# Parts of projections, merged stack transfers, earlier transposes, other engines for additions and roots, in a one-core attention kernel

## The chip, the cores and the metric

One core of one Trainium2 chip runs the program. The metric is device time in microseconds (us), the median of several executions. The engines are TensorE (PE; its weight loads are PEld), VectorE (DVE), ScalarE (ACT), GpSimd (POOL) and SyncE (SP), which here issues all transfers. TensorE's clock has two levels, 1.2 and 2.4 GHz; a granted clock of 0.50 is the lower one throughout a stretch, 1.00 the upper.

## The reference

A block of two layers with a layer norm behind each, on x of 4 batches x 2048 rows x 256, in float32:

```python
# layer 1: 16 heads of 16; the weights of a row are summed over m and multiply that row's own v
x_proj = (x @ w_in.T + b_in).reshape(b, l, 16, -1)
q, k, v = jnp.split(x_proj, 3, axis=-1)
att = softmax(jnp.einsum('blhd,bmhd->blmh', q, k) * scale, axis=2)
opt = jnp.einsum('blmh,blhd->blhd', att, v).reshape(b, l, d)
x = layernorm(x + opt @ w_out.T + b_out)
# layer 2: a router picks 4 of 16 heads of 64 for each batch
dist = softmax(jnp.mean(x @ Wr + br, axis=1)); idx = sort(top_k(dist, 4))
Qs, Ks, Vs = (x @ W + bias) of the four heads
O = softmax(Qs @ Ks.T / 8) @ Vs
x = layernorm(x + O @ Wo + bo)
```

## The kernel before, in words

**Layer 1 as tiles.** The softmax weights of a row m multiply v of row l alone, so a head needs only the largest score of a row and the sum of its exponentials. A *tile* A(b, j) is 128 rows x 1024 columns of one head: two matmuls of 96 x 512 in bf16 into a pair of PSUM banks (line 796), VectorE's minimum over 1024 columns (line 1083), ScalarE's exponential with a running sum (line 920). There are 512 tiles a batch, 32 a head. q and k stand in three bf16 levels each in a scratch tensor in DRAM, `qk_levels`; a head's operand, the *stack*, is six blocks of 16 rows for q and six for k (levels 0, 0, 0, 1, 1, 2 and 0, 1, 2, 0, 1, 0), loaded by 12 transfers (the "LS" unit, lines 566 to 579) into one of two buffers.

**Projections.** x comes in chunks of 512 rows: XT transposes a chunk on TensorE (line 769; ScalarE copies it out, line 926), QP and KP project to 128 columns of q or k (one PSUM bank, float32, line 775, read at lines 1089 and 932), VP to v (a pair of banks, 16 matmul records, line 761, read at line 1099). "LV" splits q and k into levels, on POOL or, for the first half of batch 0, on VectorE (lines 630 to 636). "SV" stores them.

**Between the layers.** When a batch's tiles are done, OT transposes, OP projects (line 761), VectorE adds and takes statistics (lines 1059 to 1069), ScalarE makes 1/sqrt(var) by a logarithm and an exponential, each with a table load ("LN", lines 972 and 974), a Newton step and the scaling follow ("NM", lines 643 to 652; VectorE, or POOL for the FO norms of batches 0 to 2), X1 transposes back. RT is the router; "LW" loads the chosen heads' weights.

**Layer 2.** Eight groups of 16 steps a batch. S is a score pair of 128 x 1024 for the row maxima (PE line 858, DVE 1162), M turns maxima into rows, T is the transposed score with the maximum taken off (PE 873 and 876, ACT exponential 990), V multiplies by the values (PE 886, accumulates four steps in one bank; ScalarE copies the bank out, line 1000, POOL adds it to `oacc`, line 726). POOL sums the exponentials (`facc`, lines 717 and 720). D sums `facc` over partitions (line 894), R spreads the reciprocal (line 901), VectorE multiplies (line 1182), FO projects (line 761). FK, FQ and FV are the projections of layer 2.

**The order.** All queues have a fixed order, worked out by `plan()`, an event simulation with a cost for every unit. `work_lists()` gives TensorE five lists, `main`, `scores`, `products`, `inputs` and `tiles`, each unit with a *spot*, a number of about the batch and its fraction. Whenever TensorE is free in the simulation, it takes among the five list heads that are ready and for which banks are free the one with the lowest spot (lines 294 to 306). PSUM is a ring of eight banks: A, S, T, XT, VP, FV, OP, FO, OT, X1 take a pair, QP, KP, FK, FQ, D, R, M one, V one for four steps. The tiles of batch b + 1 run beside layer 2 of batch b; batch 0's tiles run beside all projections of all batches (spots -1 to 0 for the tiles, 84 input units over -0.97 to -0.07); the last batch's layer 2 runs alone. The other engines take their units in the order in which the simulation made them ready.

```python
                    if n in pe_ready and (not banks_of[n] or pick(banks_of[n])):
                        key = spot
                        if best is None or key < best[0]:
                            best = (key, i, n)
```

## Time and profile before

| | |
|---|---|
| median of 3 runs | 4086.33 us (4085.86 to 4088.03) |
| the profiled execution | 4086.6 us, span 4084.8 us |
| busy PE, DVE, ACT, POOL | 3616.2, 3287.2, 3098.1, 1662.8 us |
| DVE tile minimum (line 1083) | 2048 x 1216 ns |
| ACT tile exponential (line 920) | 2048 x 1094 ns |

The page has, for each engine, the busy time and, for each group of instructions, the count, the mean duration and the idle time ahead of it with what ended it. Durations of instructions that follow one another overlap a little: back to back, VectorE's minima come every 1.11 to 1.13 us. Stages, by time: 0 to 57 start; 57 to 760 batch 0's tiles with all projections; then three times a junction and a middle (about 915 us a batch); 3490 to 3640 the last junction; then the last batch's layer 2.

### The profile page before, as it was taken

The numbers are of one execution on the slowest core, as the hardware profiler recorded it, in microseconds if no ns is written. First come the engines' busy times: TensorE is split into PE (matmuls) and PEld (weight loads), VectorE is DVE, ScalarE is ACT, GpSimd is POOL, SyncE is SP. The second block draws the span as 40 slices with busy tenths as digits, with TensorE's granted clock in tenths as the row PEclk, the third lists the DMA queues.
The fourth block names the chain that finished last, engine by engine and source line by source line (L and its number), as shares of the span: only waits on it lengthen the run. The fifth ranks groups of instructions, "written<-read, shape, count | busy, mean of one in ns | idle before, by whom it ended". The sixth has DMA issues, their size and how long they took to land.

```text
span 4084.8 us, 41654 instructions
## 1 busy us (share of the span) xinstructions
PE 3616.2 (89%) x13992; PEld 1329.7 (33%) x13992; DVE 3287.2 (80%) x3352; ACT 3098.1 (76%) x5069; POOL 1662.8 (41%) x1115
## 2 busy tenths in 40 slices
PE   7888888778999999788999999788999999599997
PEld 3233223223333333323333332323333322343443
DVE  7888888988989898888989898888989898543442
ACT  5888888886888889786888889786888889423333
POOL 3122332100445555400445545401445545437776
PEclk7777777678999999878999999778999999799998
DMA  5122221110000000210000000210000000100000
GB/s 159 67 75 67 83 75 62 57 45 16 16 16 19 21 21 26 67 38 16 16 16 19 26 16 26 73 33 16 16 16 25 21 16 19 53 9 1 11 11 11
DMA packets 117192, 142.62 MB, mean 35 GB/s; under 512 B 33394, under 2 KB 100466, under 8 KB 116978
## 3 DMA queue, kind: packets, MB, share of 16 engines
q1 hardware_dynamic: 116978, 139.95, 11.0%
q8 instruction: 112, 1.84, 0.2%
q14 instruction: 102, 0.84, 0.1%
HBM read 89.55 MB, written 50.33 MB: 34 GB/s over the span
## 4 chain that ended last, share of the span: by engine, by line
PE 47%; DVE 29%; ACT 17%; issue 5%; POOL 2%; SPq 1%; DMA 0%; POOLq 0%; DVEq 0%; ACTq 0%
DVE nmax L1083 18%; ACT ps L920 14%; PE ps L796 8%; PE ps L886 8%; PE ps L858 7%; PE ps L761 7%; PE ps L873 7%; DVE smax L1162 6%; PE ps L775 6%; POOL facc L720 2%; PE ps L876 2%; PE ps L769 1%; PE ps L894 1%; ACT probs L990 1%; DVE st L1062 1%
## 5 line engine op out<-in xcount | busy, mean ns | idle before, releaser
L920 ACT ACTIVATE ps<-ps,nmax 128x1024 f32<-128x1024 f32 x2048 | 2233.0, 1094 | 388.4 <-DVE nmax L1083 365.6
L1083 DVE TENSOR_REDUCE nmax<-ps 128x1 f32<-128x1024 f32 x2048 | 2379.4, 1216 | 135.2 <-PE ps L796 122.5
L796 PE MATMUL ps<-stack 96*128 96x512 bf16 x4096 | 1350.6, 436 | 237.0 <-ACT ps L920 149.4
L720 POOL TENSOR_TENSOR facc<-facc,probs 128x1024 f32<-128x1024 f32 x448 | 1051.2, 2346 | 550.9 <-ACT probs L990 528.8
L1162 DVE TENSOR_REDUCE smax<-ps 128x2 f32<-128x1024 f32 x512 | 616.5, 1220 | 261.3 <-PE ps L858 260.9
L796 PEld LDWEIGHTS ps<-stack 96*128 96x128 bf16 x4096 | 298.2, 102 | 1411.0 <-ACT ps L920 939.2
L990 ACT ACTIVATE probs<-ps 128x1024 f32<-128x1024 f32 x512 | 524.0, 1024 | 229.1 <-PE ps L876 227.8
L858 PE MATMUL ps<-fk,fq 64*128 64x512 f32 x2048 | 571.0, 650 | 41.4 <-ACT ps L920 38.1
L873 PE MATMUL ps<-fq,fk 64*128 64x512 f32 x2048 | 545.7, 609 | 29.0 <-ACT ps L920 27.9
L886 PE MATMUL ps<-probs,vals 128*64 128x512 f32 x2048 | 506.9, 608 | 5.0 <-ACT probs L990 4.5
L920 ACT ACTIVATION_READ_ACCUMULATOR ps<-ps,nmax 128x1 f32 x2048 | 417.0, 204 | 0.0
L873 PEld LDWEIGHTS ps<-fq,fk 64*128 64x128 f32 x2048 | 186.5, 189 | 268.4 <-issue 135.8
L858 PEld LDWEIGHTS ps<-fk,fq 64*128 64x128 f32 x2048 | 179.1, 193 | 282.9 <-ACT ps L920 150.8
L726 POOL TENSOR_TENSOR oacc<-oacc,part 128x512 f32<-128x512 f32 x96 | 121.4, 1265 | 296.6 <-ACT part L1000 296.6
L702 POOL CAST flevels<-fmax 128x8 bf16<-128x8 f32 x32 | 7.0, 219 | 547.4 <-DVE fmax L1170 547.4
L630 POOL CAST fk<-vals 128x512 bf16<-128x512 f32 x56 | 35.4, 633 | 464.3 <-DVE vals L1089 372.2
L886 PEld LDWEIGHTS ps<-probs,vals 128*64 128x64 f32 x2048 | 119.9, 136 | 264.1 <-issue 196.4
L876 PE MATMUL ps<-frows,minus 64*128 64x512 bf16 x1024 | 199.6, 380 | 0.0
L775 PE MATMUL ps<-x1T,wqk_sel 128*128 128x512 f32 x256 | 137.8, 671 | 18.1 <-DMA bqk_sel<-in_L_ffn_bq 18.1
L775 PE MATMUL ps<-fq,w_inT 128*128 128x512 f32 x256 | 139.1, 677 | 8.6 <-ACT fq L926 4.8
L717 POOL TENSOR_TENSOR facc<-probs 128x1024 f32<-128x1024 f32 x32 | 75.0, 2343 | 140.6 <-ACT probs L990 139.7
L1000 ACT ACTIVATE part<-ps 128x512 f32<-128x512 f32 x96 | 56.5, 588 | 85.5 <-PE ps L886 85.5
(117 smaller groups left out, 1985.5 us busy)
## 6 DMA issues: line engine op xcount, KB each, us to landing
stack<-qk_levels SPq DMA_DIRECT2D x768, 64.0 KB, 2.2
qk_levels<-fk SPq DMA_DIRECT2D x64, 384.0 KB, 2.6
probs<-in_L_attn_x SPq DMA_DIRECT2D x16, 512.0 KB, 3.8
res<-in_L_attn_x SPq DMA_DIRECT2D x16, 512.0 KB, 4.0
v_rows<-vals SPq DMA_DIRECT2D x16, 512.0 KB, 2.6
vrows<-v_rows SPq DMA_DIRECT2D x16, 512.0 KB, 3.4
x_rows<-y SPq DMA_DIRECT2D x16, 512.0 KB, 2.9
res<-x_rows SPq DMA_DIRECT2D x16, 512.0 KB, 3.9
```

The source lines that it names most:

```text
L720: pool.tensor_tensor(total, total, probs[:, slot, :], ALU.add).then_inc(facc_ready, 1)
L761: last = pe.matmul(ps[:, banks[t // 2], (t % 2) * D:(t % 2 + 1) * D], rowsT[:, cc, t * P:(t + 1) * P], w[:, cc, :], start=(cc == 0), stop= ...
L775: last = pe.matmul(bank(banks[0]), wT(cc), columns(cc), start=(cc == 0), stop=(cc == KC - 1))
L796: last = pe.matmul(bank(banks[i]), stack[0:SK, hd % 2, 0, t * P:(t + 1) * P], stack[0:SK, hd % 2, 1, col:col + CH], start=True, stop=True)
L858: last = pe.matmul(bank(banks[h]), fq[rows, pair, qs:qs + P], fk[rows, pair, ks:ks + CH], start=True, stop=True)
L873: pe.matmul(bank(banks[h]), fk[rows, pair, s * P:(s + 1) * P], fq[rows, pair, c * CH:(c + 1) * CH], start=True, stop=False)
L876: last = pe.matmul(bank(banks[h]), minus16[rows, :], frows[rows, g % 2, :], start=False, stop=True)
L886: last = pe.matmul(ps[rows, into, :], vals[:, s, (2 * pair + h) * FD:(2 * pair + h + 1) * FD], probs[:, (g * STEPS + s) % P_SLOTS, h * CH: ...
L920: act.activation(src, src, ACT.Exp, bias=nmax[:, b % 2, half, t, hd:hd + 1], scale=-1.0, accum_out=esum[:, b % 2, half, t, hd:hd + 1]).the ...
L990: act.activation(probs[:, (g * STEPS + s) % P_SLOTS, :].rearrange("p (h n) -> p h n", h=2), two_banks(banks), ACT.Exp, scale=float(FD) ** ...
L1083: dve.tensor_reduce(nmax[:, b % 2, half, t, hd:hd + 1], two_banks(banks), AX.XY, ALU.min).then_inc(min_ready, 1)
L1162: dve.tensor_reduce(smax[:, g % 2, s // NCH, :, s % NCH], two_banks(banks), AX.X, ALU.max).then_inc(smax_ready, 1)
```

## The change

- The projections are issued in parts: QP, KP, FK, FQ and D in 2, VP, FV, OP and FO in 4. Each part is a unit of its own in TensorE's lists, with the spot of the whole. The banks are taken by the first part; the readers wait for the last.
- A stack is loaded by 6 transfers instead of 12: for q one level is broadcast to 3, 2 and 1 blocks, for k three, two and one levels are read by one transfer.
- In batch 0's start the transposes of chunk c + 1 stand ahead of the projections of chunk c.
- In the last batch VectorE adds a V bank straight from PSUM into `oacc`; ScalarE's copy and POOL's addition go (for q = 1 to 3 of each group).
- For the FO norms of batches 0 to 2 POOL makes 1/sqrt(var) itself: a start by integer arithmetic and three Newton steps (13 operations of 128 x 4), instead of ScalarE's logarithm and exponential and one Newton step (4 operations) on POOL.
- The planner's costs change: LS 7.2 to 3.0, the POOL scaling 6.0 to 4.9, and TensorE units at spots below 0 count 1.5 times.

```diff
@@ -29,6 +29,8 @@
+NEWTON = 3
+ROOT_START = float(0x5F3759DF)
@@ -39,8 +41,12 @@
+COLD = 1.5
...
+PARTS = {"QP": 2, "KP": 2, "FK": 2, "FQ": 2, "VP": 4, "FV": 4, "OP": 4, "FO": 4, "D": 2}
@@ -64,7 +70,10 @@
-    inputs += place([u for c in chunks for u in (("XT", 0, c), ("QP", 0, 0, c), ("KP", 0, 0, c))], -3, 1)
+    ahead = [("XT", 0, 0)]
+    for c in chunks:
+        ahead += [("XT", 0, c + 1)] * (c + 1 < NCH) + [("QP", 0, 0, c), ("KP", 0, 0, c)]
+    inputs += place(ahead, -3, 1)
@@ -113,6 +122,8 @@
+    for units in (main, inputs):
+        units[:] = [(spot, u) for spot, t in units for u in [("part", i) + t for i in range(PARTS.get(t[0], 1) - 1)] + [t]]
@@ -127,9 +138,13 @@
-        name = ("PE",) + tag
-        unit(name, us, after)
-        banks_of[name], reader[name] = banks, read_by
+        parts = PARTS.get(tag[0], 1)
+        for i in range(parts):
+            name = ("PE",) + (("part", i) if i + 1 < parts else ()) + tag
+            unit(name, us / parts, after if i == 0 else [])
+            banks_of[name] = banks if i == 0 else 0
+            if i == 0:
+                reader[name] = read_by
@@ -165,7 +180,7 @@
-            unit(sp("LS", b, hd), 7.2, after + ([pe("A", k // AH, (k % AH + 1) * HEAD_TILES - 1)] if k >= 0 else []), 2.5)
+            unit(sp("LS", b, hd), 3.0, after + ([pe("A", k // AH, (k % AH + 1) * HEAD_TILES - 1)] if k >= 0 else []), 2.5)
@@ -213,7 +228,7 @@
-                    reader[pe("V", *t)] = act("V", b, g, n // BURST)
+                    reader[pe("V", *t)] = (dve if n and b + 1 == B else act)("V", b, g, n // BURST)
@@ -226,14 +241,18 @@
-                unit(act("V", b, g, q), 0.62, [pe("V", b, g, q * BURST + BURST - 1)] + free)
-                if q:
+                after = [pe("V", b, g, q * BURST + BURST - 1)]
+                if q == 0 or b + 1 < B:
+                    unit(act("V", b, g, q), 0.62, after + free)
+                if q and b + 1 < B:
                     unit(pool("V", b, g, q), 1.2, [act("V", b, g, q), act("V", b, g, 0)])
+                elif q:
+                    unit(dve("V", b, g, q), 0.69, after + [act("V", b, g, 0)])
...
-            unit(dve("R", b, g), 0.68, [pe("R", b, g), pool("V", b, g, BURSTS - 1)])
+            unit(dve("R", b, g), 0.68, [pe("R", b, g), (pool if b + 1 < B else dve)("V", b, g, BURSTS - 1)])
@@ -246,8 +265,9 @@
-        unit(act("LN", *t), 3.0, [dve(*t)])
-        unit(scale("NM", *t), 2.1 if scale is dve else 6.0, [act("LN", *t)])
+        root = act if scale is dve else pool
+        unit(root("LN", *t), 3.0, [dve(*t)])
+        unit(scale("NM", *t), 2.1 if scale is dve else 4.9, [root("LN", *t)])
@@ -306,13 +326,14 @@
+                    held[n[:1] + n[3:] if n[1] == "part" else n] = held[n]
...
-                start(n, now, cost[n] + switch)
+                start(n, now, cost[n] * (COLD if key < 0 else 1) + switch)
@@ -572,10 +594,12 @@
-                    for side, which in ((0, Q_LEVEL), (1, K_LEVEL)):
-                        for g, lv in enumerate(which):
-                            sp.dma_start(stack[g * AD:(g + 1) * AD, k % 2, side, :],
-                                         qk_dram[b, side, h, lv, r * AD:(r + 1) * AD, :]).then_inc(stack_in[k % 2], 16)
+                    rows = qk_dram[b, :, h, :, r * AD:(r + 1) * AD, :]
+                    for at, n in ((0, 3), (3, 2), (5, 1)):
+                        into = lambda side: stack[at * AD:(at + n) * AD, k % 2, side, :]
+                        lv = Q_LEVEL[at]
+                        sp.dma_start(into(0), rows[0, lv:lv + 1].to_broadcast([n, AD, L])).then_inc(stack_in[k % 2], 16)
+                        sp.dma_start(into(1), rows[1, 0:n]).then_inc(stack_in[k % 2], 16)
@@ -635,19 +659,19 @@
-        def scale_rows(eng, i, steps):
-
-            s, done = i % 2, nth_norm[i] * NEWTON_STEPS
-            r, v, n = rstd[:, s, :], var[:, s, :], newt[:, s, :]
-            eng.wait_ge(rstd_ready, i + 1)
+        def newton(eng, i, steps, done, last):
+
+            r, v, n = rstd[:, i % 2, :], var[:, i % 2, :], newt[:, i % 2, :]
...
-            eng.tensor_tensor(r, r, n, ALU.mult).then_inc(steps, 1)
-            eng.wait_ge(steps, done + 4)
+            eng.tensor_tensor(r, r, n, ALU.mult).then_inc(last, 1)
+
+        def scale_rows(eng, i):
+            s = i % 2
@@ -689,8 +713,19 @@
+                elif kind == "LN":
+                    i, base = norm_no[at], (nth[n] - 1) * ROOT_STEPS
+                    pool.wait_ge(var_ready, i + 1)
+                    if i >= 2:
+                        pool.wait_ge(n_ready[i % 2], i // 2)
+                    pool.tensor_scalar(rstd[:, i % 2, :].bitcast(I32), var[:, i % 2, :].bitcast(I32), -0.5, ROOT_START,
+                                       ALU.mult, ALU.add).then_inc(newt_pool, 1)
+                    for k in range(NEWTON):
+                        pool.wait_ge(newt_pool, base + 4 * k + 1)
+                        newton(pool, i, newt_pool, base + 4 * k + 1, root_pool if k + 1 == NEWTON else newt_pool)
                 elif kind == "NM":
-                    scale_rows(pool, norm_no[at], newt_pool)
+                    pool.wait_ge(root_pool, nth["POOL", "LN", *at])
+                    scale_rows(pool, norm_no[at])
@@ -754,14 +789,18 @@
-            def project_rows(banks, rowsT, w):
-
-                for t in range(TPC):
+            def pieces(kind, piece, count):
+                parts = PARTS.get(kind, 1)
+                return range(count * piece // parts, count * (piece + 1) // parts)
+
+            def project_rows(kind, piece, banks, rowsT, w):
+                for t in pieces(kind, piece, TPC):
...
-                last.then_inc(filled, 1)
+                if t == TPC - 1:
+                    last.then_inc(filled, 1)
@@ -770,19 +809,25 @@
-            def project(banks, wT, columns):
-                for cc in range(KC):
+            def project(kind, piece, banks, wT, columns):
+                for cc in pieces(kind, piece, KC):
                     last = pe.matmul(bank(banks[0]), wT(cc), columns(cc), start=(cc == 0), stop=(cc == KC - 1))
-                last.then_inc(filled, 1)
+                if cc == KC - 1:
+                    last.then_inc(filled, 1)
...
-                kind, at = n[1], n[2:]
-                banks = held.get(n)
+                if n[1] == "part":
+                    piece, kind, at = n[2], n[3], n[4:]
+                else:
+                    piece, kind, at = PARTS.get(n[1], 1) - 1, n[1], n[2:]
+                banks = held.get(("PE", kind) + at)
...
+                    elif was[:2] == ("DVE", "V"):
+                        pe.wait_ge(oacc_ready, sum_no(*was[2:]))
@@ -970,7 +1016,7 @@
-                    act.wait_ge(ln_ready, i + 1)
+                    act.wait_ge(ln_ready, nth[n])
@@ -1104,7 +1150,11 @@
-                    scale_rows(dve, norm_no[at], newt_dve)
+                    i = norm_no[at]
+                    dve.wait_ge(rstd_ready, nth["ACT", "LN", *at])
+                    newton(dve, i, newt_dve, (nth[n] - 1) * 4, newt_dve)
+                    dve.wait_ge(newt_dve, nth[n] * 4)
+                    scale_rows(dve, i)
@@ -1168,6 +1218,13 @@
+                elif kind == "V":
+                    b, g, q = at
+                    dve.wait_ge(pv_done, step_no(b, g, (q + 1) * BURST - 1))
+                    dve.wait_ge(part_ready, nth["ACT", "V", b, g, 0])
+                    dve.wait_ge(oacc_ready, sum_no(b, g, q) - 1)
+                    dve.tensor_tensor(oacc[:, g % 2, :], bank(held["PE", "V", b, g, q * BURST][0]), oacc[:, g % 2, :],
+                                      ALU.add).then_inc(oacc_ready, 1)
```

## Rows read from the trace of the kernel before

**Rows 1.** Busy time by stage: length, PE, PEld, DVE, ACT, POOL, granted clock, DMA share, GB/s
```profile
60.00:760.00 700.00, 607.13 (x1544) 194.57 (x1544) 621.50 (x557) 600.27 (x1062) 174.45 (x200) 0.70 0.22 71
760.00:1020.00 260.00, 205.07 (x640) 85.92 (x640) 219.02 (x261) 191.09 (x335) 24.91 (x15) 0.77 0.14 42
1020.00:1660.00 640.00, 603.18 (x2632) 199.30 (x2630) 571.19 (x532) 565.16 (x909) 332.92 (x201) 1.00 0.06 19
3640.00:4085.00 445.00, 410.46 (x1968) 177.41 (x1964) 168.09 (x209) 162.87 (x181) 324.82 (x182) 0.95 0.02 8
```

**Rows 2.** Waits of VectorE, 60 to 760 us: for whom, total us, times, longest
```profile
DVE vals L1099 <- PE ps L761: 47.5, 14, 4.4
DVE vals L1089 <- PE ps L775: 22.8, 22, 2.3
```

**Rows 3.** TensorE in order of time, 429 to 455 us: start, us, line, matmuls
```profile
429.90 6.17 PE L761 MATMUL ps<-w_inT,fq 128*128 128x256 f32 x16
...
440.88 1.23 PE L769 MATMUL ps<-ident,probs 128*128 128x128 f32 x8 [0.52 <-ACT ps L920]
442.01 6.37 PE L796 MATMUL ps<-stack 96*128 96x512 bf16 x12
448.43 3.71 PE L775 MATMUL ps<-fq,w_inT 128*128 128x512 f32 x4
451.98 1.03 PE L796 MATMUL ps<-stack 96*128 96x512 bf16 x4
452.85 1.88 PE L775 MATMUL ps<-fq,w_inT 128*128 128x512 f32 x4
```

**Rows 4.** Two rounds of a middle, 1213 to 1260 us, ACT and PE in time
```profile
1213.40 1.01 ACT L990 ACTIVATE probs<-ps 128x1024 f32<-128x1024 f32 x1
...
1232.91 1.04 ACT L990 ACTIVATE probs<-ps 128x1024 f32<-128x1024 f32 x1
...
1243.87 3.72 PE L761 MATMUL ps<-wo_sb,x1T 128*128 128x256 f32 x16
...
1250.95 0.20 ACT L972 ACTIVATE rstd<-var 128x4 f32<-128x4 f32 x1 [1.99 <-DVE var L1069]
...
1253.21 1.95 PE L894 MATMUL ps<-ones,facc 128*128 128x1 f32 x16
...
1259.07 1.02 ACT L990 ACTIVATE probs<-ps 128x1024 f32<-128x1024 f32 x1 [0.96 <-PE ps L876]
```

**Rows 5.** Waits of VectorE in the first junction, 760 to 1020 us
```profile
DVE y L1059 <- PE ps L761: 11.4, 4, 4.4
...
DVE vals L1157 <- PE ps L761: 9.9, 4, 3.8
```

**Rows 6.** TensorE in the start: projections behind a copy, the first tiles
```profile
36.73 7.11 PE L775 MATMUL ps<-fq,w_inT 128*128 128x512 f32 x16 [1.20 <-ACT fq L926]
...
57.45 1.89 PE L796 MATMUL ps<-stack 96*128 96x512 bf16 x8
```

**Rows 7.** SyncE's issues in the start: the first two stacks
```profile
48.54 11.10 SPq L577 DMA_DIRECT2D stack<-qk_levels x24
```

**Rows 8.** Page: queue with its share of 16 engines; issue with KB, us to landing
```profile
q1 hardware_dynamic: 116978, 139.95, 11.0%
...
probs<-in_L_attn_x SPq DMA_DIRECT2D x16, 512.0 KB, 3.8
```

**Rows 9.** Groups by line: busy us, mean ns | idle before, releaser
```profile
L726 POOL TENSOR_TENSOR oacc<-oacc,part 128x512 f32<-128x512 f32 x96 | 121.4, 1265 | 296.6 <-ACT part L1000 296.6
...
L972 ACT ACT_TABLE_LOAD x32 | 41.1, 1283 | 0.6
...
L643 POOL TENSOR_TENSOR newt<-rstd 128x4 f32<-128x4 f32 x12 | 2.4, 199 | 99.3 <-ACT rstd L974 99.3
```

**Rows 10.** Waits of TensorE, 3640 to 4085 us
```profile
PE ps L894 <- POOL facc L720: 16.1, 5, 9.4
```

**Rows 11.** The end: POOL's addition before its last sums; the last D
```profile
4054.57 1.26 POOL L726 TENSOR_TENSOR oacc<-oacc,part 128x512 f32<-128x512 f32 x1
...
4060.75 3.54 PE L894 MATMUL ps<-ones,facc 128*128 128x1 f32 x16 [9.43 <-POOL facc L720]
```

More of the change, by code:

```diff
@@ L469, in build @@
         order, held, freed, planned = plan()
-        fill_no = {n[1:]: i + 1 for i, n in enumerate(n for n in order["PE"] if n in held and n[1] != "V")}
+        fill_no = {n[1:]: i + 1 for i, n in enumerate(n for n in order["PE"] if n in held and n[1] not in ("V", "part"))}
         nth = {}
@@ L891, in _ @@
                         pe.wait_ge(facc_ready, add_no(b, g, STEPS - 1))
-                        for t in range(TPC):
+                        for t in pieces(kind, piece, TPC):
                             for h in range(2):
```

28 lines of the change are left out of this document (15 added, 13 removed).

## The prediction

> **What bounds the kernel now.** I read the busy shares by stage first, then who waited for whom in each stage, then the order of instructions around the pieces that the change touches. The profiled execution took 4086.6 us for a span of 4084.8; the median of the runs is 4086.33, so the two can be taken as one, and the sum below is made against 4086.6.
>
> The stages have different limits [rows 1]. In the first one (60 to 760 us: attention tiles of batch 0 beside all projections) VectorE is busy 622 of 700 us and the granted clock is 0.70, so TensorE spends most of it at 1.2 GHz. In the middle of a batch (1020 to 1660) TensorE is busy 603 of 640 us at full clock, with VectorE at 571 and ScalarE at 565: TensorE is the bound. In the last batch (3640 to 4085) it is TensorE again, 410 of 445, with POOL at 325. Between a first stage and a middle lies a junction (760 to 1020) in which nobody is above 219 of 260 us.
>
> VectorE's idle time in the first stage is 47.5 us before the 14 reads of V projections and 22.8 us before the 22 reads of Q projections [rows 2]. The rows show how it arises: a V projection of 6.17 us runs, VectorE eats the tiles that are in PSUM and stands [rows 3]. That is the loss that "other tiles between" is to remove.
>
> **The parts of the projections.** Whether a tile comes between two parts is decided by the planner, not by the chip. At each free moment it takes, of the heads of five lists, the ready one with the lowest spot; all parts of a unit get the same spot, and a tile gets in only if its own spot is lower. A V projection needs a pair of banks, as a tile does. So when one is picked, the tile at the head of its list either has a higher spot, or had no stack. It still has a higher spot when part 0 ends, and part 1 needs no bank: the four parts follow one another. The trace says that this is how these units come: between the transposes at 440.88 and the Q projection at 448.43 lie 12 tile matmuls, six tiles [rows 3], and the spots of the list (84 units over 0.9, 512 tiles over 1) put 0.9/84 x 512 = 5.5 tiles between two units. They come by their spots, not behind them. The same holds for OP and FV in the junction: their list lags behind its chain, its spots are the lowest, and nothing comes between. So the 47.5 us [rows 2] and the 11.4 and 9.9 us per junction [rows 5] stay. I cost the parts of VP, OP, FV at 0; the ends are 0 and the gain of the first rival.
>
> Units of one bank are different. After the Q projection at 448.43 two tiles follow, not 5.5, and then the next projection at 452.85 [rows 3]: it is taken ahead of its spot, because one bank is free and no pair is. Here the tile waits with a lower spot and can come after part 0. Of the 22.8 us [rows 2] the first projection of each job, which comes by its spot (2.3 us at most), keeps about 13 x 1.2 us, some 7 are left, and half of that is **-4 us** (bounds 0 and -11).
>
> In the middle, FO, FQ and D cost TensorE time whatever their order. A plain round of four T lasts from 1213.40 to 1232.91, 19.5 us, the one with FO, FQ and D from 1232.91 to 1259.07, 26.2 us [rows 4]. It is 6.7 us longer, and FO (3.72), D (1.95) and a projection (1.88 [rows 3]) alone are 7.6 us of matmuls. There is no stall in it that parts could take away: **0**. Against it: a part between S and T pairs may cost a change of shape, 0.2 us at 45 places (24 D, 21 FQ) = +9; for it: the 0.3 us a time that nine FO rounds may hold, -3.
>
> **The roots.** A root on ScalarE is two table loads and two tiny activations, 2 x (1.28 + 0.20) = 3.0 us [rows 4, 9], and ScalarE stands 1.99 us for VectorE's variance ahead of it [rows 4]. Twelve of 32 (FO of batches 0 to 2) leave ScalarE: 12 x 3 = 36 us of busy time. Nine lie in rounds that TensorE bounds, as just shown: worth 0. Three lie in the junctions, where ScalarE has slack too but a chain of norm, transpose and copy runs; I take -1 each, **-3 us** (bounds: -9 if all of it is on the chain, +3 if POOL's longer root delays the store whose buffer the second OP needs). POOL now does 13 small operations instead of 4, at 0.20 us [rows 9] and some 0.08 between, so 9 x 0.28 = +2.5 us a norm, in front of its T additions. POOL is busy 333 of 640 us there [rows 1], which hides it; if POOL were full it would be 12 x 2.5 = 30 us.
>
> **The last batch.** Each group there has three additions of 1.265 us on POOL [rows 9], 3.8 us that leave POOL. TensorE waited 16.1 us, five times, for POOL's running sum before a D [rows 10]; the last of these is 9.43 us [rows 11], the other four 6.7 us together. The four were 1.7 us each, less than the 3.8, and go. In the last group one addition of 1.26 us lies before POOL's last sums at 4054.57 [rows 11], another earlier in the same unbroken run, so the end comes 2.5 us sooner. VectorE takes them over (24 x 0.7 = 17 us of its 277 us of slack [rows 1]); an addition that stands behind an FO's statistics holds its bank some us longer. Together -9.2, less a us for that: **-8 us** (bounds -9 and -2).
>
> **The start.** Each of the four chunks stands 1.20 us between its transposes and its projections for ScalarE's copy [rows 6]. With transposes a chunk ahead three of these go, 3.6 us, less about 0.3 for the second chunk's transposes in front of the first projection: -3.3. The stack's twelve transfers are issued in 5.55 us (24 in 11.10 [rows 7]), six take 2.8. The first tile came 8.9 us after the first issue (48.54 [rows 7] to 57.45 [rows 6]). But the six are of another kind: their source is a view whose leading dimension is 3 or 2 (a broadcast level, or three levels), 192 and 128 KB long. I keep 8.9 us, between what fewer issues would save and what larger pieces may cost. The planner believes in a stack ready sooner (3.0 for 7.2 us, and projections at 1.5 times their cost), so about one V projection less is done before the first tile, and starves VectorE later, 47.5/14 = 3.4 us [rows 2]. -3.3 + 3.4 = **0** (bounds -6 and +23). Later stacks have 37 us or more from one to the next, and need not be early.
>
> **Sum.** 0 (start) - 4 (one-bank parts) + 0 (middle) - 3 (roots) - 8 (last batch) = -15: 4071.6, say **4071 us**. Its own range, by the likelier halves of the bounds, is 4050 to 4084.
>
> **Rivals.** (1) *Tiles do come between the parts of VP, OP and FV.* For it: the ring is full most of the time, and if tiles are behind their spots they win. Then a V projection of 6.17 us becomes pieces of 1.5 us, under what VectorE holds in PSUM: 14 x 2.7 = 38 us, the Q reads 8 us more than above, half of 21.3 us in each of three junctions = 32, and with the -11 of roots and last batch about -75 after what fills up elsewhere: **4011 us**. Against it: the six tiles that fit the spots.
>
> (2) *The stack's transfers run on few DMA engines.* A transfer whose leading dimension is 3 may be divided over three engines only, one of 2 over two. The first engine then gets 2 x (64 + 64 + 4) = 264 KB of a stack. The kernel's queue moved 139.95 MB in 11.0% of 16 x 4084.8 us [rows 8], 19.5 KB/us an engine: 13.5 us, and the x load's 3.8 us for 32 KB each [rows 8] leaves 2.2 fixed: 15.7 us. The first tile is at 48.54 - 3.3 + 15.7 = 60.9 instead of 57.45, and no work stands in the order to fill it: +3.5 + 3.4 = +7, **4079 us**. The Trainium skill states this rule in "DMA: Bandwidth & Descriptors", section "Why a DMA increments its semaphore by 16 and not by 1": the number of engines is the largest up to 16 that divides the slowest dimension of both sides. No row here can show it: every large transfer of this trace has 16 or 128 rows in front. By that page's 27 GiB/s an engine the 264 KB would take, as an estimate, 9.1 us, and the sum would be about 4074.
>
> (3) *The same, much slower, and the kernel is slower.* If an engine's pace with 264 KB is that of the x load as a whole (32 KB in 3.8 us [rows 8]), a stack needs 31 us: first tile 76.6, +19.2 + 3.4 = +23, **4094 us**. It decides from a landing of 24 us after the issue, where it eats the other -15. For it: TensorE's order is fixed, so a late stack stops everything. Against it: the queue's mean pace is more than twice that.
>
> **Chances.** Forecast 0.40, rival 1 0.23, rival 2 0.22, rival 3 0.15. About 0.2% (8 us) is what a measurement can tell from no change; the border is at 4078. Faster: 0.34 of the forecast's 0.40, 0.23, and 0.09 of rival 2's = 0.66. Within 0.2%: 0.06 + 0.12 = 0.18. Slower: 0.16 with rival 3 and what is left. The range for 8 in 10 runs from near rival 1 to rival 3: 4010 to 4094.
>
> **What would show it.** The V projections of the first stage still in one piece of 16 matmuls and VectorE still waiting some 45 us for them: the reading of the planner is right; tile matmuls between their matmuls, and that wait under 20: rival 1. Between the first stack issue and the first tile 9 us, 16, or 31: forecast, rivals 2 and 3. Rounds of 19.5 and 26 us in the middle: the parts and roots are worth nothing there; 24 or less refutes it. No POOL wait before D in the last batch but the last, and that one near 7. Wrong it would be above all if the new costs make the planner order the middle differently, which no row of before can show.

## Result and profile after

The changed kernel takes 4101.44 us (8 runs, 4092.38 to 4106.13) against 4086.81 us for the kernel before on the same chip: 1.0035 times as long (95% interval 1.0025 to 1.0044). It is slower by 0.35%; forecast were 4071 us and a range up to 4094.

The rows below are of one execution of 4106.1 us (span 4104.3), the longest of the eight and 4.7 above the median, so a stage difference of 19.5 us stands for 14.6 in the medians. The eight spread over 13.8 us, with a mean granted clock of 0.904 in the longest and 0.911 in the shortest; those of the kernel before spread over 3.2. First, busy time by stage in the changed kernel, columns as in [rows 1]. The junction now begins at 789 instead of 761 us, so the last three windows are set later (790 for 760, 3660 for 3640).

```profile
60.00:790.00 730.00, 562.50 (x1584) 198.91 (x1584) 633.11 (x570) 613.75 (x1068) 179.63 (x204) 0.81 0.21 69
790.00:1050.00 260.00, 207.28 (x653) 88.34 (x654) 220.42 (x261) 192.69 (x338) 24.89 (x15) 0.76 0.14 42
1050.00:1690.00 640.00, 603.32 (x2628) 197.57 (x2626) 570.17 (x532) 555.98 (x896) 340.68 (x229) 1.00 0.06 19
3660.00:4105.00 445.00, 412.13 (x1980) 178.64 (x1976) 188.46 (x235) 149.72 (x158) 296.72 (x158) 0.96 0.02 8
```

The middle and the last batch are nearly as they were. The first stage's window is set 30 us longer (by the marks below the stage is 23.8 us longer), and TensorE is less busy in it (562 against 607 us) although its granted clock rose from 0.70 to 0.81. So it is not short of TensorE; it stands.

To place the loss I read the time of marks in both traces: VectorE's first read of a tile, and in every batch VectorE's first operation of the junction (`oT<-nmax`, at 761.4 us before and 789.1 after), the routing, and the first T after it. All stretches in us; they end 3.6 us before the span in both kernels:

| stretch | before | after | difference |
|---|---|---|---|
| start to the first tile's read | 59.0 | 62.9 | +3.9 |
| first stage, batch 0 tiles to the junction | 702.4 | 726.2 | **+23.8** |
| junctions up to the routing, four | 364.5 | 369.0 | +4.5 |
| routing to the first T, four | 533.2 | 523.5 | -9.7 |
| middles, three | 3 x 658.5 | 3 x 658.2 | -0.9 |
| last batch | 446.6 | 444.5 | -2.1 |
| sum | | | +19.5 |

**The start.** Issues of the stack by SyncE, and TensorE's first tile, in the changed kernel (start us, us, engine, line; in brackets the idle time before and who ended it):

```profile
46.50 0.86 SPq L601 DMA_DIRECT2D stack<-qk_levels  x1
...
61.85 4.60 PE L841 MATMUL ps<-stack 96*128 96x512 bf16 x10 [17.70 <-DMA stack<-qk_levels]
```

(A row at the edge of its view counts only the matmuls inside it.) From the first issue to the first tile it is 15.35 us; before it was 8.9 [rows 6, 7]. Between 52 and 58 us the mean share of the 16 DMA engines is 0.19, as much as three of 16 at work all the time would give (3/16 = 0.19):

```profile
52.00:58.00 6.00, 0.00 (x0) 0.00 (x0) 0.00 (x0) 0.00 (x0) 0.00 (x0) 0.50 0.19 72
```

**The first stage.** Waits of VectorE and of TensorE between 66 and 789 us in the changed kernel (for whom, total us, times, longest):

```profile
DVE nmax L1129 <- PE ps L841: 42.8, 50, 2.6
DVE vals L1145 <- PE ps L799: 24.8, 15, 1.7
DVE vals L1135 <- PE ps L814: 24.1, 16, 1.7
```
```profile
PE ps L841 <- ACT ps L966: 119.7, 146, 2.8
PE ps L814 <- ACT ps L966: 24.2, 42, 2.8
```

and the same view of TensorE before (66 to 761 us):

```profile
PE ps L796 <- ACT ps L920: 62.9, 98, 2.2
...
PE ps L775 <- ACT ps L920: 3.3, 7, 0.5
```

VectorE waits less for V projections than in [rows 2] (24.8 against 47.5), but 42.8 us for tiles, where it was 7.3. TensorE waits 42 times in front of a Q or K projection for ScalarE to give a bank back (7 times before), and twice as long in front of tiles. TensorE in order of time around a V projection shows the pattern, the answer to [rows 3]:

```profile
445.10 1.98 PE L814 MATMUL ps<-fq,w_inT 128*128 128x512 f32 x4 [0.52 <-ACT ps L966]
446.92 0.60 PE L841 MATMUL ps<-stack 96*128 96x512 bf16 x2
448.49 1.47 PE L841 MATMUL ps<-stack 96*128 96x512 bf16 x6 [0.98 <-ACT ps L966]
450.17 0.60 PE L841 MATMUL ps<-stack 96*128 96x512 bf16 x2 [0.20 <-ACT ps L966]
451.66 0.61 PE L841 MATMUL ps<-stack 96*128 96x512 bf16 x2 [0.88 <-ACT ps L966]
452.78 3.72 PE L799 MATMUL ps<-w_inT,fq 128*128 128x256 f32 x16 [0.52 <-ACT ps L966]
456.34 2.09 PE L841 MATMUL ps<-stack 96*128 96x512 bf16 x8
```

The V projection is still one piece of 16 matmuls and the Q projection one of 4: nothing stands between parts here. What changed is that projections no longer fill the moments in which only one bank is free; each comes at its own place, behind a wait for ScalarE. The planned orders say the same for the whole stage: of the Q and K projections planned among batch 0's tiles, 37 of 50 came at least one tile ahead of their spot in the kernel before, and none of 53 does in the changed one.

**The end.** The last batch's final D in the changed kernel:

```profile
4080.65 1.63 PE L939 MATMUL ps<-ones,facc 128*128 128x1 f32 x7 [7.41 <-POOL facc L755]
```

It waited 9.43 us before [rows 11].

### The profile page after: what moved, and what is told of

It is laid out like the page before. It is cut to its first block, busy times and chain, and to the rows that moved or that the text cites. A ratio compares the mean times of both kernels' runs of the same rounds, so it can differ in the third digit from the quotient of the medians.

```text
span 4104.3 us, 41314 instructions
## 1 busy us (share of the span) xinstructions
PE 3558.5 (87%) x13992; PEld 1324.5 (32%) x13992; DVE 3313.6 (81%) x3376; ACT 3059.6 (75%) x4997; POOL 1655.9 (40%) x1199
## 4 chain that ended last, share of the span: by engine, by line
PE 47%; DVE 29%; ACT 15%; issue 4%; POOL 2%; DMA 1%; SPq 1%; POOLq 0%; DVEq 0%; ACTq 0%
DVE nmax L1129 20%; ACT ps L966 13%; PE ps L841 9%; PE ps L931 9%; PE ps L903 7%; PE ps L918 7%; PE ps L799 6%; DVE smax L1212 6%; PE ps L814 5%; POOL facc L755 2%; PE ps L921 2%; PE ps L808 1%; PE ps L939 1%; ACT probs L1036 1%; DVE st L1108 1%
## 5 line engine op out<-in xcount | busy, mean ns | idle before, releaser
L841 PE MATMUL ps<-stack 96*128 96x512 bf16 x4096 | 1289.2, 424 | 295.6 <-ACT ps L966 204.2
L841 PEld LDWEIGHTS ps<-stack 96*128 96x128 bf16 x4096 | 307.2, 102 | 1417.3 <-ACT ps L966 908.4
L918 PE MATMUL ps<-fq,fk 64*128 64x512 f32 x2048 | 545.8, 608 | 28.9 <-ACT ps L966 27.9
L761 POOL TENSOR_TENSOR oacc<-oacc,part 128x512 f32<-128x512 f32 x72 | 91.0, 1264 | 284.3 <-ACT part L1046 284.3
L814 PE MATMUL ps<-fq,w_inT 128*128 128x512 f32 x256 | 165.5, 785 | 26.9 <-ACT ps L966 24.2
L1105 DVE TENSOR_TENSOR y<-ps,res 128x1024 f32<-128x1024 f32 x32 | 39.2, 1224 | 80.8 <-PE ps L799 80.8
```

What stands on the lines that cost most here:

```text
L814: last = pe.matmul(bank(banks[0]), wT(cc), columns(cc), start=(cc == 0), stop=(cc == KC - 1))
L841: last = pe.matmul(bank(banks[i]), stack[0:SK, hd % 2, 0, t * P:(t + 1) * P], stack[0:SK, hd % 2, 1, col:col + CH], start=True, stop=True)
L918: pe.matmul(bank(banks[h]), fk[rows, pair, s * P:(s + 1) * P], fq[rows, pair, c * CH:(c + 1) * CH], start=True, stop=False)
```

## Experiments

The numbers are medians, and ratios against the kernel before on the same chip; the runs were made on several chips, on each of which the kernel before took 4086.5 to 4087.3 us. "Factor" is COLD = 1.5 on the planned cost of TensorE's units at spots below 0, that is of the start and the first stage, batch 0's tiles among them; the prediction named it only in passing.

### The shape of the six transfers

In the first experiment the same six transfers are written with their rows in front, so that the slowest dimension is 16 and not 3, 2 or 1:

```diff
-sp.dma_start(into(0), rows[0, lv:lv + 1].to_broadcast([n, AD, L])).then_inc(stack_in[k % 2], 16)
-sp.dma_start(into(1), rows[1, 0:n]).then_inc(stack_in[k % 2], 16)
+sp.dma_start(into(0), rows[0, lv].unsqueeze(1).to_broadcast([AD, n, L])).then_inc(stack_in[k % 2], 16)
+sp.dma_start(into(1), rows[1, 0:n].rearrange("v r l -> r v l")).then_inc(stack_in[k % 2], 16)
```

> The changed kernel with its six stack transfers in another division: the rows of a block are interleaved, so that 16 rows lead on both sides of each transfer (the sums over the 96 rows are in another order, nothing else changes, nor the order of any queue). Theory: in the changed kernel a stack takes 15.4 us from its first issue (46.50) to the first tile (61.85), because it runs on 3 or 2 of 16 DMA engines. Led by 16 rows it should land 6 us after the first issue, so the first tile comes at 52 to 54, 8 to 10 us sooner, and all of that stays: 4101.4 - 9 = 4092. Rival A, that the landing is set by the bytes of a transfer (192 KB) and not by its division: first tile stays at 61 to 62, time 4101. Rival B, that the few engines also hold up the other transfers of the first stage (x, levels, v): more than 10 us are won, the stage itself gets shorter, time under 4086.

Measured: 4094.89 us, 1.0019 (1.001 to 1.0028), 6.6 us under the changed kernel, where 9 were expected. The two intervals against the kernel before overlap (1.0025 to 1.0044 and 1.001 to 1.0028), so the 6.6 us are not sharply sized; the first tile is. First issue and first tile:

```profile
45.26 0.67 SPq L601 DMA_DIRECT2D stack<-qk_levels  x1
...
52.20 2.29 PE L841 MATMUL ps<-stack 96*128 96x512 bf16 x5 [7.72 <-DMA stack<-qk_levels]
```
```profile
45.00:52.00 7.00, 0.00 (x0) 0.00 (x0) 1.35 (x2) 0.00 (x0) 0.57 (x1) 0.81 0.89 210
```

Same bytes, same six transfers: 6.9 us instead of 15.35, with a DMA share of 0.89 instead of 0.19. The other way round, the kernel before with only its twelve transfers replaced by the six of the change:

> The kernel before with the six transfers of the change and nothing else (the planner's costs and all orders stay). Theory of the few engines: the first tile comes 15.4 us after the first issue at 48.5, at 63.9 instead of 57.5, and the kernel is 6 us slower, 4093; later stacks are hidden behind 37 us of tiles. If the few engines also hold up other transfers: more than 10 us slower. If the division does not matter: the first tile 2 to 3 us sooner, 4084.

Measured: 4092.21 us, 1.0015 (1.0006 to 1.0024), +5.7 us; first issue at 48.57, first tile at 63.44, 14.9 us, so the first tile comes 6.0 us later than the 57.45 of [rows 6]. Both experiments show the rival of few DMA engines at work, and in the median this edit alone costs about what the first tile is late. The profiled execution is the longest of its eleven (4096.6 us) and has another 4.5 us in the first stage; no run tells why.

### The factor on the planned costs

```diff
-COLD = 1.5
+COLD = 1.0
```

> The changed kernel with the planner's factor for units at spots below 0 back at 1.0 (was 1.5). Theory: the factor is what made the planner stop taking Q and K projections ahead of their spots; it places each by itself, 5.5 tiles apart, and each of them starves VectorE a little. With 1.0 the first stage (first tile to the end of batch 0's tiles) gets 10 to 20 us shorter, VectorE's waits for tiles there fall from 42.8 to under 15 us: 4101.4 - 15 = 4086. The first tile stays near 62. Rival: the stage is long because work of the start moved into it and because of the few-engine transfers; then the factor is worth under 4 us, 4098 or more.

Measured: 4082.02 us, 0.9989 (0.998 to 0.9998), 19.4 us under the changed kernel. The first stage is 701.7 us (726.2) in the profiled execution, which took 4075.7 us, 6.3 under this median, while that of the changed kernel was 4.7 above its own. VectorE's and TensorE's waits in it (66 to 763 us):

```profile
DVE vals L1145 <- PE ps L799: 48.9, 14, 4.3
DVE vals L1135 <- PE ps L814: 16.0, 10, 2.3
DVE nmax L1129 <- PE ps L841: 8.8, 21, 0.8
```
```profile
PE ps L841 <- ACT ps L966: 72.7, 102, 3.3
...
PE ps L814 <- ACT ps L966: 3.0, 6, 0.5
```

TensorE's waits for ScalarE in front of a Q or K projection are all but gone (3.0 us, 6 times), and 38 of 52 of these are again planned ahead of their spot. VectorE's three waits add up to 73.7 us instead of 91.7, which is 18.0 of the 24.5 us between the two stages. The factor alone, put into the kernel before:

```diff
-start(n, now, cost[n] + switch)
+start(n, now, cost[n] * (1.5 if key < 0 else 1) + switch)
```

> The kernel before with one line changed: TensorE units at spots below 0 count 1.5 times in the planner. No parts, twelve transfers. Theory: the factor alone spreads the Q and K projections and costs what it cost in the changed kernel, 15 to 20 us: 4103; the first stage's waits of VectorE for tiles rise from 7 to about 40 us, while those for the V projections fall (full clock in front of them). Rival: it hurts only together with the parts; then 4087.

Measured: 4094.54 us, 1.0028 (1.0017 to 1.0039): +8.1 us. The first tile is read 2.3 us earlier (one Q and one K projection fewer are planned ahead of it), and the first stage is 8.8 us longer, with the same sign in the planned order (none of 52 ahead of its spot) and in TensorE's waits (66 to 768 us):

```profile
PE ps L775 <- ACT ps L920: 26.0, 47, 2.8
```

Why the factor costs 19.4 us in the changed kernel and 8.1 in this one was not run down.

Factor and transfers both undone:

> Both edits together. Theory: they add up, -9 and -15: 4077, faster than the kernel before (4086.8) by 0.2 to 0.3%; the gains of the last batch, the junctions and the earlier transposes remain. Rival, that they share one cause (the idle stretch ahead of the first tile): together no better than the better of the two alone.

Measured: 4074.3 us, 0.997 (0.996 to 0.9979): 27.1 us under the changed kernel, against 6.6 and 19.4 apart. The two edits add up (26.0), and without them the rest of the change is worth 12.5 us.

### The parts

That version with no parts at all (`PARTS = {}`):

> The version with transfers led by 16 rows and factor 1.0 (4074.3), with no parts at all. In the planned order V, OP, FV and FO parts follow one another anyway; 38 of 64 Q and K projections and 39 of 64 FK and FQ have tiles between their halves. Theory: the parts are worth the one-bank pieces, 4 us in the first stage and nothing in the middle that TensorE bounds: 4078. Rival: the parts also help the middle (FQ between tiles), 10 us or more: 4085. Rival: they cost changes of shape, and without them it is faster, 4070.

Measured: 4092.69 us, 1.0016 (1.0007 to 1.0025), 18.4 us more than with parts. By stage of the two profiled executions (16.4 us apart) they bring 1.9 us in the first stage, 2.6 to 2.9 in each of three stretches from routing to the first T, 3.8 in each middle (662.2 against 658.4), and they lose 5.5 in the last batch (440.3 against 445.8). But 18 us is not the worth of the parts: the middles, and a part of the last batch, turn on the granted clock, as is shown with the roots, below.

Now the parts of the input projections (QP, KP, VP) each get a spot of their own, one tile apart, so that the planner does put tiles between; of 48 boundaries between parts of V projections 29 then have a tile in them, where it was 1:

```diff
     for units in (main, inputs):
-        units[:] = [(spot, u) for spot, t in units for u in [...]]
+        gap = 1.0 / A_TILES if units is inputs else 0
+        units[:] = [(spot + i * gap, u) for spot, t in units for i, u in enumerate([...])]
```

> As that version (4074.3), with the spots of a projection's parts one tile's spot apart in the list of inputs, so that tiles do come between the four parts of V projections. Theory of my first rival: VectorE's wait of 48.9 us for 14 V projections falls to under 20 us, the first stage gets 20 to 35 us shorter: 4045. Counter: with pieces between tiles TensorE's clock stays at 1.2 GHz, a V projection takes 6.8 us of matmuls instead of 4 to 6 and its pair of banks is missing for 10 us; then less than 10 us are won, 4066 or more.

Measured: 4057.17 us, 0.9928 (0.9915 to 0.9942), 17.1 us less. A V projection in it, in order of time (L801 V projection, L843 tiles):

```profile
288.87 1.03 PE L843 MATMUL ps<-stack 96*128 96x512 bf16 x4
289.73 1.03 PE L801 MATMUL ps<-w_inT,fq 128*128 128x256 f32 x4
290.60 0.60 PE L843 MATMUL ps<-stack 96*128 96x512 bf16 x2
291.03 1.03 PE L801 MATMUL ps<-w_inT,fq 128*128 128x256 f32 x4
292.02 0.61 PE L843 MATMUL ps<-stack 96*128 96x512 bf16 x2
```

VectorE's waits there (66 to 740 us) no longer have a V projection among the large ones:

```profile
DVE vals L1137 <- PE ps L816: 31.4, 13, 2.5
DVE nmax L1131 <- PE ps L843: 28.9, 26, 2.6
```

The first stage is 686.9 us (705.8 without the spacing). This is the mechanism of rival 1, and worth half of the 38 us that the rival gave it: a part of the wait comes back in front of tiles and Q reads (28.9 and 31.4 us, against 9.0 and 19.4 without the spacing). The same spacing for the parts of the main list too:

> As c_spread, and the parts of OP, FV, FO, FK, FQ and D spaced by a tile as well. Theory: the junctions win some of the 10 us that VectorE waits there for FV (25 of 48 parts now have a score pair or tile behind them), little for OP; the middle, bound by TensorE, wins nothing from the parts of FO: 5 to 12 us under c_spread. Rival: the switch of shape between FO's parts and V products costs 24 x 0.2 = 5 us and eats it.

Measured: 4070.89 us, 0.9962 (0.9948 to 0.9975), 13.7 us more than without. The last batch is 458.7 us instead of 444.5. V products now come between an FO's parts, and VectorE waits 25.6 us for the four FO there instead of 16.4; that is 9 of the 14 us. The middles are 2.2 us longer each, the four junctions 5.3 us shorter in all.

The last batch's units behind the attention in one piece again, input projections still spaced:

> The version with parts of the input projections one tile apart (4057.2), now with every unit of the last batch behind the attention whole (OP, FK, FQ, FV, FO, D in one piece there). The last batch was 444.5 us after its last route with parts and 440.3 without. Theory 1, that difference is the pieces' own: 4053 (4051 to 4055), and the stretch is 440. Theory 2, it came from something else that the version without parts had, such as another order before: 4056 to 4058.

Measured: **4053.22 us**, 0.9917 (0.9903 to 0.993), the fastest version of the study, 0.8% under the kernel before. The median is 4.0 us lower, as theory 1 had it, but the last batch is 443.7 us and not 440, and the two profiled executions have spans of 4051.3 and 4051.8 us. Where the 4 us come from is not shown. The 440 us of the version without parts are no proof against parts either: the last experiment with the roots has the same planned order on TensorE as this one and 3.5 us less in the last batch, where TensorE does its matmuls (one record more or less) in 3.2 us less busy time, at a higher mean clock. The last batch of this version, then of that one:

```profile
3604.60:4051.80 447.20, 414.84 (x1996) 179.69 (x1992) 190.29 (x236) 151.65 (x159) 297.33 (x158) 0.95 0.02 8
```
```profile
3619.60:4063.30 443.70, 411.64 (x1995) 178.29 (x1992) 190.18 (x236) 151.53 (x159) 296.82 (x158) 0.96 0.02 8
```

### The last batch's additions

The kernel before with this edit alone:

> The kernel before with the last batch's products added by DVE alone (no copy by ACT, no add by POOL), roots, parts, costs and transfers as before. The prediction gave this edit -8 us: 4078.5. The version without parts has its last batch 6.3 us shorter (440.3 against 446.6 us) after its last route, so theory 1 (all of that is this edit, and its batches 0 to 2 are unchanged): 4080 (4079 to 4082). Theory 2 (the adds hide, and the gain came from the earlier transposes or the roots): 4085 to 4087. If the middles of 662 us come from this edit instead, because the costs of the last batch's products shift the whole order: 4094.

Measured: 4083.77 us, 0.9991 (0.9982 to 1.0), -3.0 us. The waits before D in the last batch were 16.1 us, five times [rows 10]. Now:

```profile
PE ps L937 <- POOL facc L753: 14.1, 5, 7.4
```

Only the last one got shorter (9.43 to 7.40). The four others are 1.66 to 1.68 us long in both kernels. POOL's last additions to `facc` ahead of the first of these D show why, in the kernel before and in this one:

```profile
3673.19 4.85 POOL L720 TENSOR_TENSOR facc<-facc,probs 128x1024 f32<-128x1024 f32 x2 [0.47 <-ACT probs L990]
```
```profile
3674.27 4.85 POOL L753 TENSOR_TENSOR facc<-facc,probs 128x1024 f32<-128x1024 f32 x2 [1.70 <-ACT probs L1034]
```

In both, POOL has caught up and stands for ScalarE ahead of the last three additions; the freed time only makes that idle time longer (1.70 instead of 0.47 us).

The -3.0 us are not free of the clock. The version without parts has the same planned order in the last batch and takes 443.8 us from ScalarE's first T to the end, this kernel 446.9 and the kernel before 450.1; TensorE is busy 411.5, 414.8 and 415.7 us in them. So the edit may be worth up to 6 us where the clock holds.

### The roots, and the granted clock

The kernel before with the late roots on POOL and nothing else:

> The kernel before with the late square roots alone moved (Ln and Exp of the late norms replaced by three Newton steps on POOL; nothing in parts, twelve transfers, old costs, the sums of the last batch on ACT and POOL). The prediction gave this edit -3 us (bounds 0 and -6): 4083.5. Since then the version without parts showed, against the kernel before, each middle 3.7 us longer (662.2 against 658.5) and the last of the stretches before batch 3's routing 2.7 us longer, in sum 13.8 us, and no edit is yet named for it. Theory 1, the roots cause it, since their new costs change the planner's order at the FO rounds: 4086.5 - 0.2 x 9 + 13.8, about 4098 (4094 to 4101), middles of 662. Theory 2, the roots are hidden as the prediction said and the 13.8 us come from another edit of that version: 4083 to 4087, middles of 658.

Measured: 4100.16 us, 1.0033 (1.0021 to 1.0045): +13.4 us, middles of 662.4. The size is that of theory 1, but its reason is wrong: the order planned for TensorE, all 3924 entries, is the same in both kernels (those of ScalarE, VectorE and POOL are not). TensorE in order of time, in this kernel and in the kernel before, at the same place of batch 0's middle (16 one-column matmuls of D, then S and T):

```profile
1510.76 2.43 PE L934 MATMUL ps<-ones,facc 128*128 128x1 f32 x16
1513.12 2.08 PE L913 MATMUL ps<-fq,fk 64*128 64x512 f32 x4
1514.99 0.63 PE L916 MATMUL ps<-frows,minus 64*128 64x512 bf16 x2
1515.42 3.60 PE L898 MATMUL ps<-fk,fq 64*128 64x512 f32 x8
1518.83 1.05 PE L913 MATMUL ps<-fq,fk 64*128 64x512 f32 x4
```
```profile
1509.10 1.95 PE L894 MATMUL ps<-ones,facc 128*128 128x1 f32 x16
1510.97 1.13 PE L873 MATMUL ps<-fq,fk 64*128 64x512 f32 x4
1511.93 0.38 PE L876 MATMUL ps<-frows,minus 64*128 64x512 bf16 x2
1512.15 1.88 PE L858 MATMUL ps<-fk,fq 64*128 64x512 f32 x8
1513.87 1.02 PE L873 MATMUL ps<-fq,fk 64*128 64x512 f32 x4
```

The same instructions take twice as long for some 7 us, and then not any more. The windows of these 8 us (columns as in [rows 1], the granted clock behind the five busy times), this kernel first:

```profile
1510.80:1518.80 8.00, 8.00 (x31) 4.64 (x32) 3.01 (x4) 4.71 (x8) 1.87 (x2) 0.58 0.00 0
```
```profile
1509.10:1517.10 8.00, 8.00 (x45) 4.25 (x46) 5.59 (x7) 5.81 (x10) 2.73 (x3) 1.00 0.00 0
```

0.58 is mostly the lower of the clock's two levels. The clock falls at the same place in batches 1 and 2, and again some 90 us later in each (0.76 over 1600 to 1607 us). In the 20 us ahead TensorE did the same things with the same durations and gaps in both kernels. The version without parts has the same falls, which is where 11 of its 18 us were.

The kernel before is not free of falls: each of its middles has one, too short to show in a mean of 1.00. It too stands behind a D, whose last matmul ends at 1167.9:

```profile
1168.80:1172.00 3.20, 3.20 (x12) 1.61 (x10) 0.89 (x1) 1.73 (x3) 0.00 (x0) 0.50 0.00 0
```

The clock's records of all sixteen traces of this study say it in general. They have 82 stretches at the lower level in their 48 middles, and every one begins in the last 1.2 us of a D's one-column matmuls or at most 1.7 us behind them. A middle has seven D. The second has a fall in every one of these middles; in the kernel before it is the only one, here the last two have one too.

The best version with the roots back on ScalarE:

> The same with the late square roots back on ACT and a single Newton step on POOL, as in the kernel before. If the roots on POOL are worth the 3 us that the prediction gave them (ACT freed of two instructions and the table's loading in some 9 norms): 3 us above the version with them, about 4056. If they are worth nothing, the same within 1 us. If they cost 3.7 us in each middle in every version (the middles with parts being 658 because the parts gave back the same): 11 to 14 us below, about 4041.

Measured: 4062.75 us, 0.994 (0.9926 to 0.9953): here the roots on POOL *gain* 9.5 us. Again TensorE's planned order is unchanged (4216 entries), and again it is the clock; the middle of batch 2, roots on POOL (one fall), then on ScalarE (six falls, one at each D but the first):

```profile
2803.60:3461.80 658.20, 621.44 (x2708) 203.32 (x2704) 584.28 (x544) 570.24 (x917) 349.11 (x232) 1.00 0.07 17
```
```profile
2808.40:3476.00 667.60, 630.70 (x2708) 206.82 (x2704) 584.51 (x543) 579.03 (x929) 343.59 (x205) 0.98 0.07 17
```

TensorE is busy 9.3 us longer with the same 2708 matmuls, and the stretch is 9.4 us longer. Batch 1 has three falls and 662.0 us. Batch 0 has one fall in either version, and there the roots on POOL show what they are worth by themselves: 658.4 us against 658.9.

Does the run of one-column matmuls set it off? D goes in four pieces, and in most D one tile comes between two of the pieces (25 of 96 boundaries have one), in the kernel with the roots and in the kernel before:

```diff
-main += [(spot, ("D", b, g - 1))] * (step == 4)
+main += [(spot, (("part", step - 4) if step < 7 else ()) + ("D", b, g - 1))] * (4 <= step <= 7)
```

> The late roots alone moved, as in the version before it (4100.2), and the 16 one-column matmuls of a group's sums (D) put in four pieces of 4, which the planned order cuts by one tile in 21 of 28 groups of the middles. With D whole, the same stream of PE instructions as in the kernel before lost the full clock behind D at 1511.9 us (granted 0.58 for 8 us) and again at about 1600, in each of the three middles (662.4 against 658.5 us). Theory 1, the fall is set off by the long run of one-column matmuls, and a tile between them is enough: middles back at 658 to 659, in all 4087 (4084 to 4090). Theory 2, the fall has another cause and where D stands does not matter: middles 662 and 4100. Theory 3, any shift of the work by tenths of a us moves the falls about: middles that differ from one another.

> The kernel before with D alone in four pieces in the same way, and nothing else changed. Before has no fall behind D in its middles. Theory 1 (a tile between is harmless and only protects): 4086 to 4088, middles 658 to 659. If a cut costs PE something of its own (the array is loaded anew, another 0.3 us for each of 21 cuts): about 4090. Theory 3 (shifts move the falls about): middles with 3 to 4 us more in some batch, 4090 to 4100.

Measured: 4088.59 us (4083.79 to 4098.22) with the roots, and 4103.62 us, 1.0038 (1.0024 to 1.0051), in the kernel before. Splitting D took most of the 13 us away from the one and gave 16 to the other, whose middles are 665.6 us, with TensorE busy 626.6 us in one instead of 620.6, and with the lower clock at other places (in batch 0 from 1257 and from 1342 us). The profiled execution of the first (4098.2, middles of 664.0) is 9 us above the highest of its ten others, and its mean granted clock is 0.887 where theirs is 0.888 to 0.890; that fits falls that differ between executions of one kernel, but only one execution was profiled. In both traces each middle has three falls, again each at the end of a D or behind it, though these D are in pieces: a tile between pieces does not protect. The clock is as long at the lower level there as in the middles of 662.4 us with D whole (some 14 us of each), so some of the 7 us per middle of the second kernel can be the pieces' own cost; that was not separated.

So a D is where the clock falls in a middle, in one piece or in four. Whether its one-column matmuls do it, or what stands around them, is not shown, since no run is without D; and at which of the seven D it falls is left open. Shown is that this changes under one and the same TensorE order, and that it carried 13.4 us in one pair of kernels and most of 9.5 us in another.

## Why the prediction was wrong

**The planner's factor (the failed step).** "The planner believes in a stack ready sooner (3.0 for 7.2 us, and projections at 1.5 times their cost), so about one V projection less is done before the first tile": +3.4 us. Even the count ahead of the tile was low: the planned order has one V, one Q and two K projections less there. Above all, the factor holds for every unit of the first stage, and reorders 700 us of it. In the changed kernel it costs 19.4 us, in the kernel before 8.1. The text even named "if the new costs make the planner order the middle differently" as what would upset it, looked for it in the middle, and gave it no chance; it was in the first stage. There the old order had projections in the gaps in which one bank is free and no pair is, the very thing the prediction had read in [rows 3] for its -4; with the factor none of them is ahead of its spot any more.

**The transfers (rival 2 in place of the forecast).** I kept 8.9 us for the landing; it is 15.35, and rival 2 said 15.7. First tile: rival 2 said 60.9, measured 61.85. For the landing alone rival 2 had 15.7 - 8.9 = +6.8 us; measured are +5.7 (the kernel before with the six) and 6.6 (the changed kernel with the other six). The Trainium skill ("DMA: Bandwidth & Descriptors", section "Why a DMA increments its semaphore by 16 and not by 1") has the rule that the number of engines is the largest up to 16 that divides the slowest dimension of both sides. These runs agree with it: with 3, 2 or 1 in front the mean share is 0.19, with 16 in front 0.89. The estimate of 9.1 us that the prediction made from that page's bandwidth of an engine is below the measured 14.9 and 15.35 us, and the measurement decides. Nor are six issues as quick as the 2.8 us that the prediction had: they take 3.9 (46.50 to 50.42; twelve took 5.55). The step that failed here is the 8.9 us kept between two ends of which only one, rival 2, had a mechanism.

**Transposes ahead, -3.3.** About right, though it was not run alone. In the nine traces with it the first stack issue comes at 44.6 to 46.5 us (median 45.09), in the seven without at 48.1 to 49.8 (48.57). The factor does not move it in the kernel before (48.52).

**Parts of two-bank units, 0.** Right: no tile came between. What would happen if one did was right in kind (rival 1), 19 us in the first stage and not 38.

**One-bank parts, -4.** With the factor off, the Q waits fall from 22.8 to 16.0 us, but the stage by 0.7 only (702.4 to 701.7). The gain came elsewhere: FK and FQ parts between the routing and the first T, 2.6 to 2.9 us in each of three batches, for which the sum had no term.

**Middles, 0.** 658.5 against 658.2 in the changed kernel: right there, with one fall of the clock in each middle of both. But it holds only while there are no more falls, and the bounds (+9, -3) rested on changes of shape and stalls; the 0.2 us for a change of shape had no row beside it (four T matmuls take 1.13 us behind the D at 1509.10 and 1.02 behind the S before 1513.87). The term that was missing is 4 us per middle with three falls and 9 with six, in a stage where [rows 1] shows a mean of 1.00.

**Roots, -3.** Where the clock is alike they are worth 0.5 us a middle (batch 0 of the best version: 658.4 against 658.9, with 26.19 instead of 26.39 us for a round with an FO). Alone they measured +13.4, in the best version -9.5, nearly all of it by the clock.

**The last batch, -8.** Measured -3.0 alone (-2.1 by stage in the changed kernel), perhaps 6 with the clock of the version without parts. The end term was right: 2.5 said, 2.0 measured, "near 7" said, 7.41 measured. Wrong was that four waits of 1.7 us before D would go because POOL does 3.8 us less per group. They are 1.66 to 1.68 with either amount of work: POOL has caught up with ScalarE three additions before the D, and from there on it has the same to do, three additions of some 2.4 us and four small operations. A wait that is the same each time is not shortened by work that the engine had finished before it.

With measured sizes the sum is +6.6 (transfers) + 19.4 (factor) - 12.5 (what is left of the change, 4086.8 to 4074.3) = +13.5, against +14.6 measured. The term that the forecast had for the factor, +3.4, measured +19.4, and its 0 for the landing measured +6.6. What is left is near the forecast's -15, but not by its terms: the last batch gave less than its -8, the Q reads and the roots almost nothing, and the routing stretches gave 8 to 9 us that it did not have.

## What to carry to other kernels

Where an order is computed from costs, a changed cost is an edit of its own: run it alone before you credit what it was to support. When transfers are merged, look at which dimension stands in front, not only at their number. And give every splitting a spot of its own; parts of equal priority stay one piece.

## What the runs showed of the hardware

With six transfers of the same 768 KB the first tile came 6.9 us after the first issue with 16 rows in front and 14.9 to 15.4 us after it with 3, 2 or 1 in front. In a stage that TensorE bounds at 0.94 busy, the granted clock fell to 0.58 for 8 us behind a D in one kernel and not in another with the same order on TensorE, and a batch's middle came out at 658, 662, 666 or 668 us, most of it by that. All 82 falls in the middles of the sixteen traces begin in the last 1.2 us of a D's one-column matmuls or at most 1.7 us behind them. Differences below some 15 us in this kernel (0.4%) are not read as the worth of an edit unless the clock of the stretches is compared too.
